# The last image group loaded in the early slot, group 1 in the late one

## What is computed

```python
x = x + conv(gn(x))           # gn: zero mean, unit variance of each (image, channel)
                              # conv: + bias[c], each pixel repeated 2x2, a 12x12 low-pass filter,
                              # leaky_relu(0.2) * sqrt(2), a second 12x12 filter, every 2nd row and column
t = x.reshape(16, 1024, 32)
t = t + attention(ln(t))      # one head, width 32, causal, softmax over 1024 keys
t = t + experts(ln(t))        # 16 experts: softmax of the gate over the tokens, top 8 tokens of each,
                              # pooled, two small layers with gelu, scattered back
return t.reshape(x.shape)
```

## Time and profile before

| | |
|---|---|
| median of 3 runs | 408.36 us |
| lowest, highest of them | 402.58, 410.03 us |
| time of the profiled execution | 402.22 us |
| its span, first to last instruction | 400.3 us |
| PE busy | 348.1 us, 87% |
| DVE busy | 306.9 us, 77% |
| ACT busy | 258.9 us, 65% |
| POOL busy | 239.5 us, 60% |

### The profile page before, as it was taken

The page is one execution under the profiler, slowest core; times in us unless marked ns, Lnnn a source line. Parts: engine busy times, 40 slices in busy tenths (PEclk is TensorE's granted clock), DMA queues, the critical chain, the costliest instruction groups (busy, mean ns, idle before and its releaser), DMA issues.

```text
span 400.3 us, 7849 instructions
## 1 busy us (share of the span) xinstructions
PE 348.1 (87%) x3046; PEld 260.0 (65%) x3046; DVE 306.9 (77%) x558; ACT 258.9 (65%) x347; POOL 239.5 (60%) x141
## 2 busy tenths in 40 slices
PE   1299999999899999999599999999986887979775
PEld 1188867667687676757477677686764545646675
DVE  3777879777969878699769786986998995766621
ACT  1132453897987959698476788898696887832500
POOL 5234454386678798787635989756497975153000
PEclk9999999999999999999799999999998997998755
DMA  4810000000000000000000000000020000000311
GB/s 142 169 25 1 2 2 0 3 2 0 3 2 2 2 0 3 2 1 2 0 2 2 2 2 2 2 2 2 0 55 1 3 0 25 19 0 2 106 53 52
DMA packets 16193, 6.93 MB, mean 17 GB/s; under 512 B 6767, under 2 KB 16029, under 8 KB 16157
## 3 DMA queue, kind: packets, MB, share of 16 engines
q1 hardware_dynamic: 13440, 5.78, 5.5%
q10 hardware_dynamic: 2717, 0.66, 1.1%
HBM read 3.63 MB, written 2.11 MB: 14 GB/s over the span
## 4 chain that ended last, share of the span: by engine, by line
PE 57%; DVE 15%; ACT 10%; issue 9%; DMA 4%; POOL 3%; ACTq 1%; SPq 0%; DVEq 0%; POOLq 0%
PE psB L912 13%; PE psA L912 11%; PE psB L1028 5%; ACT Pp L602 5%; PE psA L1013 4%; PE psB L1049 4%; PE psA L1095 3%; DVE negmax L770 3%; PE psA L902 3%; PE psA L1057 3%; PE psA L1073 2%; DVE Pp L395 2%; DMA x_all<-in_x_dram 1%; POOL Pp L395 1%; DVE xin L713 1%
## 5 line engine op out<-in xcount | busy, mean ns | idle before, releaser
L395 POOL TENSOR_TENSOR Pp<-e,Pp 128x1024 f16<-128x1024 f32 x45 | 107.4, 2393 | 11.7 <-ACT Pp L602 11.5
L770 DVE TENSOR_REDUCE negmax<-psA 128x1 f32<-128x512 f32 (+7 forms) x128 | 90.7, 750 | 18.3 <-PE psA L1016 17.6
L601 ACT ACTIVATE e<-psB 128x1024 f32<-128x1024 f32 (+1 forms) x80 | 76.6, 957 | 9.9 <-PE psB L1031 4.6
L602 ACT ACTIVATE Pp<-psB 128x1024 f16<-128x1024 f32 (+1 forms) x80 | 76.8, 960 | 0.0
L912 PE MATMUL psB<-xin,UU 128*128 128x224 f16 (+1 forms) x480 | 56.3, 276 | 1.1 <-ACT Pp L602 0.6
L1013 PE MATMUL psA<-zK,yQ 128*128 128x512 f16 (+1 forms) x192 | 49.1, 339 | 9.1 <-DVE uT L790 4.9
L912 PE MATMUL psA<-y,DD 128*128 128x224 f16 (+1 forms) x480 | 55.1, 273 | 0.0
L1028 PE MATMUL psB<-yQ,zK 128*128 128x512 f16 (+1 forms) x192 | 49.1, 335 | 6.9 <-ACT Pp L602 3.5
L912 PEld LDWEIGHTS psB<-xin,UU 128*128 128x128 f16 x480 | 46.7, 99 | 9.8 <-ACT oT L606 1.5
L912 PEld LDWEIGHTS psA<-y,DD 128*128 128x128 f16 x480 | 46.8, 98 | 5.5
L481 POOL TENSOR_TENSOR zrstd<-zrstd,power 128x8 f32<-128x8 f32 x16 | 26.3, 1643 | 29.9 <-DVE zrstd L750 29.6
(11 more groups left out here) (164 smaller groups left out, 602.6 us busy)
## 6 DMA issues: line engine op xcount, KB each, us to landing
x_all<-in_x_dram SPq DMA_DIRECT2D x4, 512.0 KB, 4.1
out_dram<-x_all SPq DMA_DIRECT2D x8, 256.0 KB, 2.3
yQ<-rows SPq DMA_DIRECT2D x32, 2.0 KB
Pp<-filter_tables ACTq DMA_DIRECT2D x4, 121.9 KB, 4.2
w_halves<-y SPq DMA_DIRECT2D x12, 32.0 KB, 1.8
cst<-shape_constants SPq DMA_DIRECT2D x1, 326.5 KB, 4.2
y<-in_L_ffn_weight_dram SPq DMA_DIRECT2D x4, 64.0 KB, 2.1
xin<-in_L_ffn_weight_dram SPq DMA_DIRECT2D x1, 256.0 KB, 3.5
```

The costliest lines, as they stand in the source:

```text
L395: return engine.tensor_tensor(Pp[:, n % 2, 1, o:o + N], e32[:, (NU * n + i) % 3, 0:N], Pp[:, n % 2, 0, o:o + N], ALU.subtract)
L601: nc.scalar.activation(e32[:, m % 3, 0:N], slot(e)[:, 0:N], ACT.Exp)
L602: nc.scalar.activation(Pp[:, n % 2, 0, UOFF[e[2]]:UOFF[e[2]] + N], slot(e)[:, 0:N], ACT.Exp).then_inc(b_drained, 1)
L770: ins = nc.vector.tensor_reduce(negmax[:, n % 2, m - 1:m], s[:, at:at + P * m], X, ALU.max, negate=True)
```

## The change

SP's list of transfers is changed in two places. The group that is loaded right behind the small weights is now the last one, group 3 (`G - 1`), and the loop behind the wait for the tables now loads groups 1 and 2 in place of 2 and 3. The three transfers have one size and one form, and each group's semaphore goes with it.

```diff
-            sp.dma_start(x_all[:, 1, :].rearrange("p (b a n) -> p b a n", b=GB, a=2), x_tokens[1]).then_inc(x_loaded[1], 16)
+            sp.dma_start(x_all[:, G - 1, :].rearrange("p (b a n) -> p b a n", b=GB, a=2), x_tokens[G - 1]).then_inc(x_loaded[G - 1], 16)
             sp.wait_ge(toeplitz_loaded, 16 * R)
-            for g in range(2, G):
+            for g in range(1, G - 1):
                 sp.dma_start(x_all[:, g, :].rearrange("p (b a n) -> p b a n", b=GB, a=2), x_tokens[g]).then_inc(x_loaded[g], 16)
```

## The result

| | before | changed |
|---|---|---|
| median of 4 runs | 405.47 us | 409.22 us |
| lowest, highest | 402.29, 410.03 | 403.89, 412.68 |
| ratio of the comparison | | 1.0111, 95% interval 1.0056 to 1.0165 |
| span of the profiled execution | 400.3 | 410.7 |

The changed kernel is slower, by about 1%. I had forecast no change. Which sort an execution becomes turned out to be the question.

A forecast was written before the change was run, and what follows sets the result against it. PE, busy 87% of the span, was taken to bound the kernel. The 2.6 us wait removed, less 2.6 us idle opened, gave 0, so the median of 408.36 stayed: 408.3 us, range 401.5 to 411.8.

The forecast's parts named there:

- which the weight loads had given away: At `up 0`, first weights came at 21.87, 0.43 us after the transposes' weight loads, so the unmoved `UU` transfer decided: gain 0.
- The reading of the chain of waits: At the start, the 5.38 us load of group 3 is on the chain, but a second releaser arrives simultaneously: gain 0.
- The cover on DVE's side: DVE's work up to 35.90 us isn't started by `up 0`, so `up 0` up to 0.53 us earlier would wait there.
- the one on the clock: At the first `up`, its f16 matmuls likely raise the clock near 24.3 us, not the f32 transposes; rise unmoved.
- the slower rival: At the first `up`, the clock rises later after PE's idle stretch: some +2 us, at most +4.9, time 410.4; chance 0.10.
- my reading of the last 25 us: From 376 to 386 us, PE is busy 7.9 of 10 us on f32 work, yet the granted clock stays at 0.50.
- The third rival: At PE's 4.08 us wait for DVE at 192 us, a start shifted by tenths opens or closes a stall: 404 or 412; chance 0.08.

The follow-up runs named there:

- the held kernel: Changed kernel, with PE holding the transposes of group 3 until group 2 has landed, against the kernel before: median 404.31 us, ratio 1.0002.
- the doses behind the first `up`: Needless f16 matmuls between first and second `up`: kernel before with 3 or 9, medians 404.24 and 408.91 us; changed kernel with 7 or 3, 405.79 and 404.16.
- the ten times with seven matmuls: Changed kernel with seven needless f16 matmuls between first and second `up`: ten single times, median 405.79 us, ratio 1.0079 to the kernel before.

## Why the prediction was wrong

**Right, step by step.** The load lands early, and the transposes start at 17.4; the wait of 2.6 us in front of them goes and one of 2.7 us comes behind; `up 0` is released by the transfer into `UU`, which the weight loads had given away; groups 1 and 2 are waited for by nobody; the load order itself costs nothing (the held kernel, 1.0002). The reading of the chain of waits, that its 5.4 us of load were not worth anything, holds. The cover on DVE's side does not. I had put down that an earlier `up` would wait for DVE before the sum for image 0; with the transposes done twice the first `up` ended 0.9 us earlier (25.54 against 26.45) and the sum came at 34.91 in place of 35.82. DVE's L733, 1.46 us in the kernel before and 0.34 there, ended in both within 0.14 us of the end of POOL's L503, which itself waits for ACT's eviction of the first `up`. So that part of DVE's chain does follow the first `up`.

**The step that failed** is the one on the clock. The prediction named it as the slower rival, with the price "some +2 us if only the first `up` is hit", and gave it 0.10. Its sign, a first `up` of over 5.5 us, is what the profile shows (5.95). I had argued it down, since the f32 work from 376 to 386 us does not raise the clock; "so the f16 matmuls of `up` are likely what raised it". The transposes done twice refute that: the clock rose inside them. Work on f32 in one place of the kernel was not a measure for other work in another place. Why it stays at half in 376 to 386 I haven't tested; those products use 64 rows of the array and the transposes of group 3 use 128, and PE waits more there. And the 4.02 us that I read as solid work are a poor measure of it. The same 16 matmuls took as long a little earlier in the kernel before, where the granted clock was 1.00; first PE's timeline, then the stretch:

```profile
366.60 4.00 PE L1095 MATMUL psA<-obd,xF_all 64*128 64x128 f32 x16
```
```profile
366.00:370.00 4.00, 4.00 (x22) 3.83 (x19) 2.71 (x2) 0.00 (x0) 0.00 (x0) 1.00 0.02 4
```

Twice the clock made them no faster (4.00 against 4.02), while eight transposes went from 1.97 to 1.10. So a PE that the profile calls busy there is held by something other than its clock; by what, no run shows.

Sized: with the transposes directly ahead of it the first `up` took 4.55, 4.87, 5.45, 4.88 and 4.82 us (the kernel before and its variants that leave the place alone, and the held one; mean 4.9), with the gap 5.95, 6.07, 6.23, 6.21, 6.18 and 4.84 (mean 5.9). The gap costs about 1.0 us at the start, so the rival's +2 us for the first `up` was too much and its sign right. The length is a matter of chance in both, with another mean.

The Trainium skill (TensorE: Matmul & The Clock Gate, Part 1: The HAM clock gate) says that PE's activity releases the half rate, and names no type of data. The runs agree with that section and not with my reading of the last 25 us: 3.37 us for sixteen f32 transposes. The page as a whole does set transposes apart, which the prediction left out: its section Part 4: PE-mode transpose says of them that full rate "doesn't engage". Here the measurement decides, and the clock rose inside them. Its sentence that for modelling the ramp penalty is "<1% of a typical kernel span" also holds for the 1.0 us at the start, but not for what hangs on it here.

**The term that was missing** is larger. The third rival, "a shift of tenths changes a later meeting", had the right form, but I placed it at a wait at 192 us for DVE, gave it 0.08, and took it as possible only if the start moved. It is the meeting of the clock's falls with the stretch behind 282 us, where PE waits often. The executions of the kernel before are long in 39 of 79 cases, those of the changed one in 13 of 14. With 402.3 and 409.4 as means of the two sorts, 0.44 more long ones are 0.44 x 7.1 = 3.1 us; the long ones of the changed kernel are themselves 0.7 us longer (410.1), as the later start has it, and the sum is about the 3.9 us between the means. That the shift itself does it, and not chance, is shown by the doses behind the first `up`, above all by the ten times with seven matmuls, which came out as named beforehand; the distance in the table above says which way it works. That a start 0.7 to 0.9 us better gave no clearly faster kernel, three times over, says the same.

What stays open: why 261 us from the rise to that `pool` is the good distance, since the table rests on one profile of each kernel and was not tested, and where each fall near the end begins. A fill that does stand ahead of the fall at 286 us was not run. The median of 408.36 that I started from was itself made of both sorts; with 79 times the kernel before has 403.8. My point of 408.3 came near the measured 409.22 for the wrong reason.

## What to carry to other kernels

A load on the chain of waits is worth nothing if a second input arrives with it; look at the weight loads, which tell which one held the matmuls. PE work that can stand in a wait is worth more directly in front of the long run of matmuls that follows than as early as it can run: here it was worth 1.0 us of the first 30 matmuls. Before an idea from the profile is tested by a fill, look in the new profile whether the fill stands where it was meant to. And where executions of one kernel fall into sorts, compare the share of each before and after, with many single times; an edit of a microsecond can move the share and cost four.

## What the runs showed of the hardware

- f32 transposes of 128 x 128, with only a few small f32 products ahead of them, brought the clock from 1.2 to 2.4 GHz: sixteen in 3.37 us, where eight at 1.2 GHz take 1.97 and at 2.4 GHz 1.10.
- 2.7 us of idle PE in front of the first long run of matmuls moved the rise inside it by about 2 us (5.9 against 4.9 us for 30 matmuls, of which each us at half clock costs half).
- The granted clock reads 1.00 over the first 40 us of both kernels, although PE works at half rate there up to the rise (eight transposes in 1.94 or 1.97 us against 1.10). At the start only the durations tell it.
- 16 f32 products with 64 rows and 128 columns took 4.00 us at a granted clock of 1.00 and 4.02 at 0.50.
- The mean granted clock tells the two sorts of the kernel before apart in all four groups: 0.943 or 0.944 in the short executions, 0.919 to 0.931 in the long ones.
- The executions of one kernel on one core fell into two sorts 7 us apart (means 402.3 and 409.4 us). 1.5 us of needless matmuls made a kernel of 409.7 us 3.9 us faster.
- DVE's L733 took 1.46 us in the kernel before, 2.18 in the changed one and 0.34 with the transposes done twice, and ended each time 0.13 or 0.14 us behind POOL's L503, which ran beside it.
